# A pipelined perceiver layer on one core: the second layer norm moved ahead of the first maximum, v made apart from q and k, and the order of all three engines rewritten around it

## What is computed

```python
# 1: latent cross attention, 16 heads, 32 latent columns
C_q = LN(x) @ Wq_d; C_kv = ctx @ Wkv_d
scores = einsum('bnhl,bkl->bhnk', (C_q @ W_qk).reshape(b, n, 16, 32), C_kv) / sqrt(32)
x = x + einsum('bhnk,bkhd->bnhd', softmax(scores), (C_kv @ Wv_u).reshape(...))
# 2: self attention, one head of 128
q, k, v = LN(x) @ Wqkv + bqkv
x = x + (softmax(q k^T / sqrt(128)) @ v) @ Wo + bo
# 3: Hadamard + 4-bit rows, times ternary weight
xh = LN(x) @ hadamard; s = max(|xh|, per row) / 7
x = x + (clip(round(xh / s), -8, 7) * s) @ ternary(weight).T
```

## Time and profile before

| | |
|---|---|
| median of 3 runs | 356.9 us (356.89 to 359.89) |
| the profiled execution | 358.43 us, of which its span 356.6 us |
| PE busy | 308.3 us, 86% |
| DVE busy | 251.1 us, 70% |
| ACT busy | 191.7 us, 54% |
| POOL busy | 93.1 us, 26% |
| mean granted TensorE clock | 0.960 |

### The profile page before, as it was taken

One profiled execution on the slowest core, in us unless ns is written; L12 is line 12 of the kernel. 1 busy time (PEld: TensorE's weight loads), 2 busy tenths in 40 slices (PEclk: granted clock), 3 DMA queues, 4 the chain that ended last, 5 costly groups with the idle time before them and its releaser, 6 DMA issues.

```text
span 356.6 us, 11424 instructions
## 1 busy us (share of the span) xinstructions
PE 308.3 (86%) x4612; PEld 203.9 (57%) x4612; DVE 251.1 (70%) x530; ACT 191.7 (54%) x629; POOL 93.1 (26%) x133
## 2 busy tenths in 40 slices
PE   5766759999798999899999999999999999968871
PEld 3445447665456566666666565657575666645520
DVE  1454883878587787778787878788787878767432
ACT  1360652847547483829384756657484839282210
POOL 2004232323212221314132323222222223131321
PEclk9995687999999999999999999999999999998997
DMA  7980210303113130303040312213132020000000
GB/s 219 332 304 2 67 54 8 113 4 93 56 35 119 33 118 31 118 29 118 3 141 3 102 45 51 96 29 118 31 119 63 2 61 2 33 2 31 0 31 29
DMA packets 13345, 25.37 MB, mean 71 GB/s; under 512 B 3200, under 2 KB 3712, under 8 KB 13312
## 3 DMA queue, kind: packets, MB, share of 16 engines
q1 hardware_dynamic: 13312, 24.91, 21.5%
HBM read 20.71 MB, written 4.19 MB: 70 GB/s over the span
## 4 chain that ended last, share of the span: by engine, by line
PE 35%; DVE 25%; ACT 24%; issue 11%; POOL 2%; DMA 1%; POOLq 0%; DVEq 0%; ACTq 0%
ACT prob L313 11%; DVE mx L435 10%; PE ps L716 9%; PE ps L612 6%; PE ps L722 5%; PE ps L730 4%; DVE nmx L439 3%; ACT prob L310 3%; PE ps L737 3%; DVE stat L464 3%; DVE stat L483 3%; PE ps L706 2%; POOL rstd L267 2%; ACT q_t L301 2%; ACT p2t L301 2%
## 5 line engine op out<-in xcount | busy, mean ns | idle before, releaser
L310 ACT ACTIVATE prob<-ps,nmx,qk_scale 128x128 f32<-128x128 f32 x128 | 56.7, 457 | 39.5 <-DVE nmx L439 39.5
L622 PE MATMUL ps<-had_s,x3t 128*128 128x512 f32 x128 | 59.2, 606 | 1.4 <-ACT x3t L301 1.4
L313 ACT ACTIVATE prob<-ps,nmx,qk_scale 128x128 f32<-128x128 f32 x128 | 48.5, 489 | 0.0
L435 DVE TENSOR_REDUCE mx<-ps 128x8 f32<-128x1024 f32 x32 | 39.0, 1220 | 10.0 <-PE ps L612 10.0
L445 DVE STREAM_TRANSPOSE prob_t<-prob 128x1024 f32<-128x1024 f32 x32 | 39.1, 1223 | 6.9 <-ACT prob L313 6.9
L294 POOL TENSOR_TENSOR res<-prod,x 128x512 f32<-128x512 f32 x16 | 20.2, 1264 | 82.0 <-DVE prod L549 82.0
L622 PEld LDWEIGHTS ps<-had_s,x3t 128*128 128x128 f32 x128 | 23.0, 190 | 27.2 <-issue 25.3
L655 PEld LDWEIGHTS ps<-x2t,wqkv_s 128*128 128x128 f32 x256 | 30.9, 198 | 10.4 <-ACT x2t L301 10.4
L716 PE MATMUL ps<-prob_t,ckv_n 32*32 32x128 f32 x2048 | 33.1, 300 | 4.0 <-DVE prob_t L445 2.5
L655 PE MATMUL ps<-x2t,wqkv_s 128*128 128x128 f32 x256 | 33.9, 288 | 2.9 <-ACT x2t L301 1.4
L259 POOL TENSOR_TENSOR rstd<-aux,power 128x1 f32<-128x1 f32 x16 | 8.8, 548 | 91.5 <-DVE aux L470 91.5
(11 more groups left out here) (112 smaller groups left out, 559.7 us busy)
## 6 DMA issues: line engine op xcount, KB each, us to landing
ct<-ctx_cols SPq DMA_DIRECT2D x16, 512.0 KB, 4.0
xt<-x_cols SPq DMA_DIRECT2D x16, 256.0 KB, 2.7
xr<-x_rows SPq DMA_DIRECT2D x16, 256.0 KB, 2.7
y<-res SPq DMA_DIRECT2D x16, 256.0 KB, 3.6
w_rows<-weight SPq DMA_DIRECT2D x1, 1024.0 KB, 7.9
had_s<-hadamard SPq DMA_DIRECT2D x1, 1024.0 KB, 7.0
wqkv_s<-wqkv SPq DMA_DIRECT2D x1, 768.0 KB, 8.3
wqk<-w_qk SPq DMA_DIRECT2D x2, 128.0 KB, 4.5
```

The lines of the kernel that those rows point to most:

```text
L310: last = nc.scalar.activation(prob[:, h, :], score, ACT.Exp, bias=nmx[:, h:h + 1], scale=scale, accum_out=sum_a[:, h:h + 1])
L313: last = nc.scalar.activation(prob[:, h, :], score, ACT.Exp, bias=nmx[:, h:h + 1], scale=scale)
L435: V.tensor_reduce(mx[:, h], ps[:, 2 * half:2 * half + 2, :].rearrange("p r (c k) -> p (r c) k", c=EC), AX.X, ALU.max).then_inc(done["mx"], 1)
L622: mm = pe.matmul(ps[:, B4, :], x3t[:, c, :], had_s[:, c, :], start=(c == 0), stop=(c == EC - 1))
```

## The change

It adds and removes no arithmetic; it reorders three engines and splits two steps.

- DVE: the second norm (L464 to L470) now stands before the maxima. The maxima come in three steps, heads 0 to 3, heads 4 to 7, and heads 8 to 15, the last behind the third norm and ahead of amax. mx2 and nmx2 stand ahead of qi_t, and x3 stands right behind `turned(1)`, rsum2 ahead of it; sum, qscale, rsum and prod follow.
- ACT: heads 0 to 3, x2t, heads 4, 5, lat, z, heads 6, 7, q2 and k2, heads 8 to 10, p2, v2, p2t, heads 11, 12, o2t, heads 13 to 15, q_t, ckv, u_t, and then x3t of the next turn.
- PE: scores, Hadamard product, x2n turned, latent q, latent kv, q and k, `qt`, `s2`, qi turned, v, p2 turned, half the integer product, `o2t`, the other half, `wo`, `ckv`, `u`, x3 turned, `xo`.
- Set-up: the bias row and two of the four ternary chunks go to the end of turn 0 on DVE, the other two chunks stay in turn 1; `wide_scale` goes from turn 0 to turn 1; `hadamard_mean` and both halves of `ternary_transposed` stand later in turn 1.
- Semaphore qkv is split into qk and v.

```diff
+                if isinstance(i, int) and i == 1:
...
+                    copy(scale_row[:], ps[:, B4, :]).then_inc(row_read, 1)
                 if cross:
                     after(act, made["pt"], i - 1)
                     after(act, done["rsum"], i - 1)
-                    after(act, done["nmx"], i * 2)
-                    exps(0, 6)
+                    after(act, done["nmx"], i * 3)
+                    exps(0, 4)
...
-                if isinstance(i, int) and i == 1:
-                    act.wait_ge(hmean_made, 1)
-                    copy(had_sum[:, 0, :], ps[:, B4, :]).then_inc(hmean_read, 1)
-                if cross:
-                    exps(6, 8).then_inc(done["exp"], 1)
+                if cross:
+                    after(act, done["nmx"], i * 3 + 1)
+                    exps(4, 6)
                 if front:
                     after(act, made["lat"], i + 1)
                     copy(lat[:], ps[:, B3, 0:P + 2 * SKV]).then_inc(read["lat"], 1)
...
                     nc.scalar.activation(z[:], ps[:, B4, :], ACT.Identity, bias=round_c[:], scale=qinv[:])\
...
-                if cross:
-                    after(act, done["sum"], i - 1)
-                    after(act, done["nmx"], i * 2 + 1)
-                    exps(8, 11)
...
+                if isinstance(i, int) and i == 1:
+                    act.wait_ge(hmean_made, 1)
+                    copy(had_sum[:, 0, :], ps[:, B4, :]).then_inc(hmean_read, 1)
+                if cross:
+                    exps(6, 8).then_inc(done["exp"], 1)
+                if self_:
+                    after(act, made["qk"], i - 1)
...
-                    after(act, made["o2t"], i - 2)
-                    copy(v2[:], ps[:, B1, 2 * P:3 * P]).then_inc(read["qkv"], 1)
-                if cross:
-                    exps(11, 16).then_inc(done["exp"], 1)
+                if cross:
+                    after(act, done["sum"], i - 1)
+                    after(act, done["nmx"], i * 3 + 2)
+                    exps(8, 11)
...
                     nc.scalar.activation(p2[:], ps[:, B3, 0:SQ], ACT.Exp, bias=nmx2[:], scale=float(D2) ** -0.5,
                                          accum_out=sum2[:]).then_inc(done["exp2"], 1)
-                if front:
-                    after(act, made["qt"], i + 1)
-                    copy(q_t[:], ps[:, B2, :].rearrange("p (c b q) -> p b c q", c=EC, b=2)).then_inc(read["qt"], 1)
-                if isinstance(i, int) and i == 1:
...
-                if front:
-                    after(act, made["ckv"], i + 1)
-                    copy(ckv[:, 1 - par], ps[:, B1, 0:2 * SKV]).then_inc(read["ckv"], 1)
-                if self_:
+                if self_:
+                    after(act, made["v"], i - 1)
+                    after(act, made["o2t"], i - 2)
+                    copy(v2[:], ps[:, B1, 2 * P:3 * P]).then_inc(read["v"], 1)
...
                         last = copy(p2t[h, h], ps[h, B3, h])
                     last.then_inc(read["p2t"], 1)
+                if cross:
+                    exps(11, 13)
+                if self_:
                     after(act, made["o2t"], i - 1)
                     after(act, made["wo"], i - 2)
                     copy(o2t[:], ps[:, B3, 0:P]).then_inc(read["o2t"], 1)
+                if cross:
+                    exps(13, 16).then_inc(done["exp"], 1)
+                if front:
+                    after(act, made["qt"], i + 1)
+                    copy(q_t[:], ps[:, B2, :].rearrange("p (c b q) -> p b c q", c=EC, b=2)).then_inc(read["qt"], 1)
+                    after(act, made["ckv"], i + 1)
+                    copy(ckv[:, 1 - par], ps[:, B1, 0:2 * SKV]).then_inc(read["ckv"], 1)
...
+                if cross:
+                    after(act, made["u"], i)
...
+                    copy(u_t[:].rearrange("p c (b q) -> p b c q", b=4),
+                         ps[:, 0:4, 0:P].rearrange("p b (c q) -> p b c q", c=EC)).then_inc(read["u"], 1)
...
-            def ternary():
+            def ternary(chunks):
...
-                for c in range(EC):
+                for c in chunks:
...
-                def largest(half):
-
-                    h = slice(8 * half, 8 * half + 8)
-                    V.tensor_reduce(mx[:, h], ps[:, 2 * half:2 * half + 2, :].rearrange("p r (c k) -> p (r c) k", c=EC),
+                def largest(n, r0, r1):
...
+                    h = slice(4 * r0, 4 * r1)
+                    V.tensor_reduce(mx[:, h], ps[:, r0:r1, :].rearrange("p r (c k) -> p (r c) k", c=EC),
...
-                if cross:
-                    after(dve, made["s"], i)
-                    largest(0)
...
                 if cross:
-                    largest(1)
...
-                    ternary_scale()
-                    dve.wait_ge(cb_made, 1)
-                    V.tensor_tensor(const_row[:], ps[:, B4, :], bo_row[:], ALU.add).then_inc(const_ready, 1)
-                if isinstance(i, int) and i == 1:
-                    ternary()
+                    after(dve, made["s"], i)
+                    largest(0, 0, 1)
+                    largest(1, 1, 2)
...
                     V.tensor_scalar(aux3[:], mv3[:, 1:2], EPS, None, ALU.add).then_inc(done["aux3"], 1)
-
+                if cross:
+                    largest(2, 2, 4)
...
+                    ternary_scale()
+                if isinstance(i, int) and i == 1:
+                    ternary((2, 3))
...
                     after(dve, made["had"], i - 2)
                     V.tensor_reduce(amax[:], ps[:, B4, :], AX.X, ALU.max, apply_absolute_value=True)\
...
-                if quant:
-                    after(dve, made["qit"], i - 2)
-                    V.tensor_scalar(qi_t[:], qit_bank.rearrange("p (c t) -> p c t", c=EC), QMIN, None, ALU.max)\
-                        .then_inc(read["qit"], 1)
                 if self_:
                     after(dve, made["s2"], i - 1)
                     V.tensor_reduce(mx2[:], ps[:, B3, 0:SQ], AX.X, ALU.max).then_inc(done["mx2"], 1)
...
                     V.tensor_scalar(nmx2[:], mx2[:], -float(D2) ** -0.5, None, ALU.mult).then_inc(done["nmx2"], 1)
+                if quant:
+                    after(dve, made["qit"], i - 2)
+                    V.tensor_scalar(qi_t[:], qit_bank.rearrange("p (c t) -> p c t", c=EC), QMIN, None, ALU.max)\
...
+                if self_:
+                    after(dve, done["exp2"], i - 1)
...
+                    V.reciprocal(rsum2[:], sum2[:]).then_inc(done["rsum2"], 1)
                 if cross:
                     turned(1).then_inc(made["pt"], 1)
+                if self_:
+                    after(dve, made["wo"], i - 1)
...
+                    V.scalar_tensor_tensor(x3[:, 1 - par], ps[:, B3, :], rsum2[:], x2b[:], ALU.mult, ALU.add)\
...
                 if cross:
                     after(dve, done["rsum"], i - 1)
                     V.tensor_reduce(sum_a[:, 8:16], prob[:, 8:16, :], AX.X, ALU.add).then_inc(done["sum"], 1)
...
+                if isinstance(i, int) and i == 0:
+                    dve.wait_ge(cb_made, 1)
+                    V.tensor_tensor(const_row[:], ps[:, B4, :], bo_row[:], ALU.add).then_inc(const_ready, 1)
+                    ternary((0, 1))
...
                 if first and i == 1:
-                    hadamard_mean()
+                    wide_scale()
+                if self_ and quant:
+                    after(pe, done["x2n"], i - 1)
...
+                        mm = pe.transpose(ps[:, B2, c * P:(c + 1) * P], x2n[:, c * P:(c + 1) * P], ident[:])
+                    mm.then_inc(made["x2t"], 1)
                 if front:
...
                     mm.then_inc(made["lat"], 1)
...
+                if first and i == 1:
+                    hadamard_mean()
...
-                    for s in range(3):
+                    for s in range(2):
...
-                    mm.then_inc(made["qkv"], 1)
-                if quant:
-                    after(pe, done["qi"], i - 2)
...
-                        mm = pe.transpose(qit_bank[:, c * P:(c + 1) * P], qi[:, c * P:(c + 1) * P], ident_b[:])
...
+                    mm.then_inc(made["qk"], 1)
...
                     mm.then_inc(made["qt"], 1)
-                if first and i == 1:
-                    ternary_transposed(0)
                 if self_:
                     after(pe, read["qk"], i - 1)
...
                         mm = pe.matmul(ps[h, B3, 0:SQ], q2[:, h], k2[:, h], start=True, stop=True)
                     mm.then_inc(made["s2"], 1)
-                if front:
...
-                    pe.matmul(ps[:, B1, 0:2 * SKV], fold4[:].rearrange("p r l -> p (r l)"), lat[:, P:P + 2 * SKV],
...
-                if first and i == 0:
-                    wide_bias()
-                    wide_scale()
...
+                if quant:
+                    after(pe, done["qi"], i - 2)
...
+                        mm = pe.transpose(qit_bank[:, c * P:(c + 1) * P], qi[:, c * P:(c + 1) * P], ident_b[:])
+                    mm.then_inc(made["qit"], 1)
+                if self_:
...
```

(47 more changed lines are left out.)

88 lines of the change are left out of this document (32 added, 56 removed).

## The result

The changed kernel takes 405.1 us (median of 4 runs, 402.9 to 407.2) and the kernel before 357.6 us beside it (356.9 to 359.9): 1.132 times as long, with an interval of 1.123 to 1.140. The forecast was 393, in a range of 380 to 405: the median lies on the upper edge of the range (with the 356.9 that the forecast started from, the ratio gives 404). The profiled execution took 407.2 us, 48.8 more than that of before. Some executions of a kernel are slower as a whole than its others; the ratios leave them out, so that a ratio can differ a little from that of the medians.

The account below looks back on a forecast made before the run. A turn was taken as close to PE's own work, with one chain round all engines. 13 turns longer by 3.4 us, less POOL's hold in two, gave +42.5; set-up -6.8, drain +0.8: +36.5, 393 us, range 380 to 405.

Parts of the forecast that it names:

- The main step: ACT waits 1 to 1.6 us for z with heads 6, 7 queued behind; `turned(0)` at 10.90 instead of 8.4.
- POOL's hold of the third nmx: POOL's x2b holds DVE's third nmx until it ends; 0.83 us taken, bounds 0 to 1.1; forecast's chance 0.38.
- no hold: Rival: POOL's x2b does not delay the third nmx; 2.55 us more a turn, 383 us; chance 0.22.
- From `turned(0)` to p2: DVE's order kept, mx2 at 13.41, p2 on ACT at 13.86; heads 11 to 15 now wait behind p2.
- From p2 to `u`: p2's turning, p2t, heads 11 to 15 and `turned(1)` lead from p2 at 13.86 to `u` at 18.62.
- the clock's rival: PE's clock falls behind a thin stretch each turn, near 0.9 us; 399 to 405 us; chance 0.25.
- The tail: From `u` to the next scores 3.57 us instead of 4.5, with `wo` and `ckv` ahead of `u`.
- 0.9 us given away: Second norm ahead of the maxima on DVE moves the first exponential to 3.83 from 2.9.
- Faster: Rival: PE runs without stalls at 17.9 us a turn if z and p2 never make ACT wait; 339 us; chance 0.07.
- no difference: Rival: ACT's waits cost about 0.5 us a turn and the set-up pays for it; 357 us; chance 0.04.
- Set-up: Work moved out of DVE's way in turns 0 and 1 wins 6.8 us, bounds 3 and 8.
- drain: Turns 15 and 16 at the end together cost 0.8 us more, bounds -1 and +3.

Follow-up runs that it names:

- e1: Changed kernel with the exponentials of heads 6 and 7 ahead of z again on ACT: 377.4 us, 1.055 times the kernel before.
- g2: Kernel before with one edit, the exponentials of heads 6 and 7 behind z: 379.3 us, 1.058 times the kernel before.
- e2: Changed kernel with POOL making x2b behind qk_scale, away from the third nmx: 390.4 us, 1.091 times the kernel before.
- f3: f2 with heads 8 to 15 in one piece ahead of p2 on ACT and rsum2 behind `turned(1)`: 364.0 us, 1.015 times the kernel before.
- g3: f2 with the next pair's first norm moved behind mx2 and qi_t on DVE: 354.2 us, 0.987 times the kernel before.
- f2: Changed kernel with heads 6 and 7 ahead of z and x2b behind qk_scale: 360.9 us, 1.007 times the kernel before.
- e3: Changed kernel making the product `qt` three times in turns 2 to 14, filling PE's gap: 398.1 us, 1.116 times the kernel before.
- g4: g3 with x3 turned behind `xo` again, at the end of the turn: 359.9 us, 0.999 times the kernel before.
- f1: Changed kernel with the first two maxima ahead of the second norm and x2b behind qk_scale: 390.8 us, 1.088 times the kernel before.
- f4: Kernel before with only the set-up spread as in the change, `ternary_transposed` left in place: 354.6 us, 0.983 times the kernel before.
- g1: The kernel before with only the set-up spread, run again with more executions: 352.3 us, 0.983 times the kernel before.
- e4: Changed kernel with the first two maxima ahead of the second norm again, third maximum unmoved: 391.5 us, 1.094 times the kernel before.

## Why the prediction was right, and where it was short

**The main step held.** "Heads 6, 7 stand behind z", so that ACT waits for qinv while DVE waits for ACT: forecast z at 9.14 and `turned(0)` at 10.90, measured 9.16 and 10.85. Shown by taking it out (e1, -28 us) and by putting it alone into the old order (g2, +21 us).

**POOL's hold of the third nmx held**, nearly in size too. Forecast start 6.95 and end 8.02; measured 6.95 and 8.03. I took 0.83 in 11 of 13 turns, 9.1 us; z was late in 12 of them, by 11.2 us in sum (changed kernel against e2). The whole effect of e2, 1.05 a turn or 13.7 us, has the clock's share in it. The rival "no hold" (383) is out: the hold is there, and without it this kernel stands at 390.

**From `turned(0)` to p2 held**: mx2 13.41 forecast and 13.39 measured, p2 13.86 and 13.83. That heads 11 to 15 wait behind p2 held as a wait, but it wasn't the only one: f3 shows PE's queue waiting for p2 as well. Of what the stretch costs, the first norm's place between qi and mx2 is 0.6 us a turn in the middle of the loop (g3 19.30, f2 19.93): p2 comes 0.94 earlier without it, `u` 0.63.

**From p2 to `u` the sum failed.** I had 4.76 us (13.86 to 18.62); turn 13 has 5.76 (13.83 to 19.59), and the other turns 5.2 to 5.8, turn 4 alone 4.84. The terms at full clock were right, as e3 shows (4.84, `u` at 18.68). At the low level p2's turning takes 0.48 and not 0.33, the first half of the integer product, which stands ahead of `o2t`, 1.04 (a half takes 0.59 in g3), `wo` 1.91 (1.12) and `ckv` 1.06 (0.59). I priced the clock as a rival, at 0.9 a turn and a chance of 0.25, where it should have been a term of the sum: forecast and rival both came true. This is the largest part of the way from 393 to 405, and that the range held it is owed to the clock's rival, whose upper end set the range's. The Trainium skill ("TensorE: Matmul & The Clock Gate", HAM oscillation — how this bites in real kernels) describes a loop whose waits, there for DMA, send the clock down in every round; the row with 0.58 us of work in 3.40, and the clock of 0.62 and 0.50 behind it, agree, here with waits for other engines. My argument against it, that stretches as thin had kept the full clock in the rest of the trace, was wrong: in turn 13 of the kernel before PE is idle for 0.88 us in all, in the thinnest 3.4 us of any turn from 2 to 14 it has 1.9 us of work or more, and in the thinner stretches of turns 0, 1 and 15 the clock did fall. Here it is idle for 2.82 in one stretch, and about as long in every turn but 4.

**The tail held.** `u` to the next scores 3.57 forecast; 3.73 in all turns of the loop, 4.04 in turn 13, where `u` itself takes 2.20 and not 1.90, its start still at the low level. What g4 adds: its gain is not in the chain (0.1 a turn) but in PE's gap.

**"0.9 us given away" by the second norm was no cost.** First exponential 3.83 forecast, 3.84 measured, but the heads that `turned(0)` waits for stand behind z, and z did not come earlier with the maxima first (f1).

**The other rivals.** Faster needed qinv by 7.5, and it is there at 8.91; no difference needed a cost of 0.5 a turn, and it is 4.1.

**Set-up and drain.** Set-up -8.5 where I took -6.8, past its bound of -8: right in kind, and alone worth 6 us (f4, g1); the rest may come with the order of turns 0 and 1, which was not tried. The drain cost +3.5 and not +0.8, past its bound of +3. It was not tried by itself; 2.3 of it go with heads 6 and 7 ahead of z (49.5 in e1, and 51.8) and 2.6 with the maxima first (49.2 in e4), so its cause stays open. Open, too, is turn 3, ahead of the entry of the loop: it takes 25.84 us here, 22.9 in g3 and 20.6 before, with idle time within `u` that the profile puts down to "issue", which names no releaser. In e3 (22.42) and f3 (19.85) that idle time is missing.

**The sum by what was shown:** of the 4.1 us that a turn grew, the heads behind z are 1.5 in the chain, POOL's hold 0.86, the first norm's place 0.6, the clock 0.5. Read as steps between kernels, clock included: e1 and e2 together take off 2.97 (23.20 to 20.23), g3's move of the first norm 0.54 (19.69), and 0.62 are left to the 19.07 of before. No run shows what these last are; the split of v and the new order of the integer product's halves were not tried by themselves, so that they cost and bring nothing stays unproven.

**What the forecast was short of:** the span grew by 48.7 and not by 36.5, 12.2 more. The drain is 2.7 of them, the set-up -1.7, the turns 11.2: turn 3 took 1.8 more than its share, the other twelve 9.4, of which the clock is some 6, the tail 1.9 and the hold 2.1 (these three overlap a little).

## What to carry to other kernels

An instruction that waits in an in-order queue takes all behind it along: before moving independent work behind one, work out when the awaited value will be there, not only whether the engine is idle. Two short waits of different engines can make one gap on PE, and once that gap has nearly no work in it, add the lower clock to the sum as a term of its own; here filling the gap with work that nobody needs was a gain. When a change is many edits, try the ones that touch only one stage by themselves: here the set-up's part was a gain of 1.7% in the middle of a loss of 13%, and two swaps were nearly all of the loss.
